# Convolution halves moved into the outer turns of a window attention, and the attention leads of TensorE's program set to one offset in a block of 256 instructions

## The chip, the cores and the metric

One core of one Trainium2 chip runs the whole program. The metric is the time of an execution on the device in microseconds (us). TensorE (PE), VectorE (DVE), ScalarE (ACT), GpSimd (POOL) and SyncE (SP) each run a program of their own and meet only in semaphores.

## The reference, cut to what matters

Eight images of 256 channels and 56 x 56 pixels go through two layers, both of the form `x = x + f(group_norm(x))`, in float32:

```
x = x + conv3x3(gn(x))                       # 256 -> 256 channels
qkv    = einsum('nchw,oc->nohw', windows(gn(x)), qkv_w)   # windows of 4 x 4 pixels
pooled = 5 x 5 average of qkv inside the window
q, k   = relu(q), relu(k) ; v = [v, 1]       # 32 + 32 heads of 8, plain and pooled
kv     = einsum('ngld,nglm->ngdm', k, v)
out    = einsum('ngld,ngdm->nglm', q, kv) ; out = out[..., :-1] / out[..., -1:]
x = x + batch_norm(einsum('nchw,oc->nohw', out, proj_w))
```

## The kernel before

**Convolution.** An image is cut into 4 chunks of 14 rows (`c`). Along a row the 3 taps become 4 products (`kk`, Winograd's F(2,3)), so an image has 16 steps; `v = 16 * image + 4 * c + kk` numbers them. A step is two halves (`mt`, output channels 0 to 127 and 128 to 255); `product(v, mt)` (L320) issues one half: 18 matmuls of 128 x 392 on split float32 operands. VectorE forms the step's input `dt` (`product_inputs`), ScalarE rounds it to `dp`'s high part (`split`), VectorE subtracts for the low part (`low_parts`), and later adds the half from PSUM to the image (`add_product`, semaphore `conv_added`). `conv_bank` (L87) names each half's PSUM bank.

**Attention.** An image has 196 windows, 8 to a tile, so 25 tiles. `attention(b)` runs 25 turns, s = 0 to 24. In turn s TensorE (`tile`, L417) does: `attend` of tile s (64 small float32 matmuls, issued as 128 pairs of a weight load and a matmul); `keys_times_values` of tile s+1 (64 pairs); `q_of_tile` of tile s+2 (8 pairs); `turn`, four transposes of tile s, after VectorE's `outputs`; `pooled` of tile s+2 (2 pairs, after VectorE's `kv_low_part`); `project` of tile s-1 (16 pairs, after VectorE's `mask`); `keys_values` of tile s+3 (6 pairs). The first and the last turns leave out what has no tile. Turns 1 to 20 are a hardware loop (`pe.Fori`) of two turns a pass; turn 0 ahead of it and turns 21 to 24 behind it are written out, and so is all convolution.

**How the two are woven.** The first chunk of the next image's convolution (steps 0 to 3) is issued by `first_chunk(b)` between the group norm and the first small products of image b's attention: a part of this, from `product(v + 3, 0)` to the entry of the loop, is called the lead here. Two halves of the next step, (c, kk) = (1, 0), stand in turns 23 and 24, where `q_of_tile` has nothing to do. The remaining halves follow in `later_chunks`. The last image's attention has no convolution beside it. VectorE's and ScalarE's programs have the same weave in `first_chunk`, `attention` and `later_chunks`.

**Instruction slots.** A pair of a weight load and a matmul is two instructions. Waits that do not fit on one are instructions of their own: some 7 in a turn, the loop's own included. From one lead to the next TensorE's program as written has 4,238 instructions, and 4,238 = 16 x 256 + 142.

**Loads.** SP stores each image row group when its tiles are added, and after row group 11 (all tiles to 20 are in) it loads the image after next into the freed rows.

Of the kernel before, what the change touches and what calls it, by code (L numbers as in the profile page):

```python
# [76 lines left out]
BANK_Q = 0  # L77
# [9 lines left out]
def conv_bank(v, mt):  # L87

    c, kk = v // len(PRODUCTS) % CONV_CHUNKS, v % len(PRODUCTS)
    if (c, kk) == (0, len(PRODUCTS) - 1):  # L90
        return BANK_O + mt
    if (c, kk) == (1, 0):
        return (BANK_Q, BANK_KV)[mt]
    return BANK_C[kk % 2][mt]
# [23 lines left out]
FIRST_LOOPED = 1  # L118

# [11 lines left out]
def build(nc, x, w_conv, w_q, w_kv, w_proj, bn, gavg, pool_m, ident, hmask, vinit, out):  # L131
    ctx = ExitStack()
    with ctx:
# [182 lines left out]
        def _(pe):  # L316
# [101 lines left out]
            def tile(T, e, s=None, v=None):  # L418
# [30 lines left out]
                if is_tile(2):  # L449
                    pe.wait_ge(q_ready, n2)  # L450
                    q_of_tile(e)
                if v is not None and not is_tile(2):
                    if is_tile(1):
                        pe.wait_ge(q_ready, n2)
                        product(v, 0)
                    else:
                        pe.wait_ge(vp_raw, n1)
                        product(v, 1)
                pe.wait_ge(ao_ready, n1)
                turn(units(0))  # L460
                if is_tile(2):
                    pooled(n3)
                if is_tile(-1):
                    if is_tile(1):
                        pe.wait_ge(masked, own_mask)
                    else:
                        pe.wait_ge(y_ready, n0)
                    project(1 - e, 2)
                if is_tile(3):
                    pe.wait_ge(xh_low, n4)  # L470
                    pe.wait_ge(vp_raw, n3)
                    keys_values(n4, 1 - e)
# [9 lines left out]
            def attention(b):  # L482
                t0 = b * TILES
                v = (b + 1) * CONV_STEPS + len(PRODUCTS) if b + 1 < B else None
                pe.wait_ge(q_ready, t0 + 1)
                q_of_tile(1)
                if b + 1 == B:
                    first_keys_times_values(b)
                pe.wait_ge(xh_low, t0 + 3)
                pe.wait_ge(vp_raw, t0 + 2)  # L490
                keys_values(t0 + 3, 0)
                if b + 1 < B:
                    pe.wait_ge(conv_added, 2 * v + 4)
                for s in range(FIRST_LOOPED):
                    tile(t0 + s, s % 2, s)
                with pe.Fori(0, LOOPED // 2) as i:
                    for e in range(2):
                        tile(t0 + i * 2 + (FIRST_LOOPED + e), (FIRST_LOOPED + e) % 2)
                for s in range(FIRST_LOOPED + LOOPED, TILES):
                    tile(t0 + s, s % 2, s, v)  # L500
# [17 lines left out]
            def later_chunks(b):  # L518

                for c in range(1, CONV_CHUNKS):
                    for kk in range(len(PRODUCTS)):
# [3 lines left out]
                        if b >= 1 and (c, kk) == (1, 2):  # L526
                            pe.wait_ge(y_ready, b * TILES + 1)
                        product(v, 0)
                        if b >= 1 and (c, kk) == (1, 1):
                            last_tile(b - 1)  # L530
# [6 lines left out]
            def first_chunk(b):  # L537
# [12 lines left out]
                second_tile(b)  # L550
                product(v + 3, 0)
# [3 lines left out]
                product(v + 3, 1)  # L555
# [30 lines left out]
        def _(act):  # L586
# [73 lines left out]
            def attention(b):  # L660
                for s in range(-1, TILES):
                    if s >= 0:
                        turned(b, s)
# [22 lines left out]
            def first_chunk(b):  # L686
# [13 lines left out]
                split(v + 5)  # L700
# [37 lines left out]
        def _(dve):  # L738
# [104 lines left out]
            def later_chunks(b):  # L843
                for c in range(1, CONV_CHUNKS):
                    for kk in range(len(PRODUCTS)):
                        v = b * CONV_STEPS + c * len(PRODUCTS) + kk
                        at = (c, kk) if b + 1 < B else None
                        low_parts(v + 1)
# [19 lines left out]
            def first_chunk(b):  # L868
# [36 lines left out]
                add_product(v + 3, 1)  # L905
# [65 lines left out]
            def attention(b):  # L971
                normalize_tile(b, 3)
                tile_low(b, 3)
                for s in range(TILES):
                    weights(b, s)
                    outputs(b, s)
                    if s + 2 < TILES:
                        kv_low_part(b, s + 2)
                    if s + 1 < TILES:
                        mask(b, s + 1, 0)  # L980
                        mask(b, s + 1, 1)
                        pooled_q(b, s + 1)
                    if s + 4 < TILES:
# [225 lines left out]
```

## Time and profile before

| | |
|---|---|
| median of 3 executions | 2502.22 us (2491.29 to 2502.49) |
| the profiled execution's own time | 2488.01 us |
| its span, first to last instruction | 2486.1 us |
| TensorE busy | 2389.9 us, 96% |
| VectorE busy | 1970.8 us, 79% |
| ScalarE, GpSimd busy | 1280.5 us, 1169.2 us |
| TensorE's mean granted clock | 0.994 of full |

The profiled execution is 0.6% under the median of the three others and 0.1% under the fastest of them. Busy time is that in which an instruction of the engine was running by the record.

### The profile page before, as it was taken

Reading aid. Unit: us, or ns where it says so; the run is one execution under the profiler, and the core shown is the slowest. Engines: PE = TensorE matmul, PEld = TensorE weight load, DVE = VectorE, ACT = ScalarE, POOL = GpSimd, SP = SyncE. Lnnn points to the kernel's source line nnn. Section 1 sums busy time; section 2 is a strip of 40 time slices with the busy share of each in tenths; the row PEclk is TensorE's granted clock in tenths of the full one; section 3 lists DMA queues with packets and bytes.
Section 4 is the critical chain, followed back from the end, with each engine's and each line's share of the span. In section 5 each row is a group of like instructions: output and inputs, shape, how many; then the busy total and the mean of one; then the engine's idle time right before and its main releaser. Section 6 shows DMA issues by size and latency. Waiting matters only on the chain.

```text
span 2486.1 us, 112351 instructions
## 1 busy us (share of the span) xinstructions
PE 2389.9 (96%) x49576; PEld 2162.7 (87%) x49576; DVE 1970.8 (79%) x3608; ACT 1280.5 (52%) x3352; POOL 1169.2 (47%) x2364
## 2 busy tenths in 40 slices
PE   4999999999999999999999999999999999999998
PEld 4998889888898888988889888898889978898887
DVE  8887868888688886878858788687886878865886
ACT  2137751377514774157731577316772267722775
POOL 0026760277503775047740477305772067712776
PEclk9999999999999999999999999999999999999999
DMA  4000010000100002000010000100001000000000
GB/s 166 1 2 14 17 61 16 2 16 15 65 12 2 16 19 72 1 2 19 19 68 1 6 15 19 69 1 6 19 15 69 1 9 15 21 11 2 16 15 24
DMA packets 38959, 58.19 MB, mean 23 GB/s; under 512 B 4688, under 2 KB 36304, under 8 KB 36560
## 3 DMA queue, kind: packets, MB, share of 16 engines
q1 hardware_dynamic: 38736, 55.27, 6.3%
q8 instruction: 133, 2.18, 0.4%
q14 instruction: 90, 0.74, 0.1%
HBM read 29.57 MB, written 25.69 MB: 22 GB/s over the span
## 4 chain that ended last, share of the span: by engine, by line
PE 95%; issue 2%; DVE 1%; ACT 0%; DMA 0%; POOL 0%; SPq 0%; POOLq 0%; DVEq 0%
PE ps L334 34%; PE ps L405 15%; PE ps L353 11%; PE ps L394 10%; PE ps L380 9%; PE ps L360 9%; PE ps L369 4%; PE ps L414 3%; DMA xs<-w_conv 0%; PE ps L319 0%; DVE st L772 0%; PE ps L561 0%; PE ps L345 0%; ACT ve L613 0%; DVE xh L914 0%
## 5 line engine op out<-in xcount | busy, mean ns | idle before, releaser
L334 PE MATMUL ps<-dp,wc 128*128 128x392 f32 x4608 | 844.7, 343 | 5.6 <-issue 5.6
L334 PEld LDWEIGHTS ps<-dp,wc 128*128 128x128 f32 x4608 | 821.0, 189 | 11.3 <-issue 9.7
L1138 POOL TENSOR_TENSOR ve<-vpraw,vmask 128x1024 f32<-128x1024 f32 x200 | 392.1, 1961 | 364.6 <-ACT vpraw L624 364.6
L405 PEld LDWEIGHTS ps<-at,wp 128*128 128x128 f32 x3200 | 376.3, 192 | 49.6 <-DVE kvm L954 46.3
L1109 POOL TENSOR_TENSOR qm<-qraw 128x64 f32<-128x64 f32 x200 | 59.5, 298 | 763.2 <-ACT qraw L631 763.2
L914 DVE TENSOR_SCALAR xh<-xs,gn 128x128 f32<-128x128 f32 (+3 forms) x560 | 407.9, 781 | 0.5 <-PE ps L360 0.2
L405 PE MATMUL ps<-at,wp 128*128 128x128 f32 (+1 forms) x3200 | 405.5, 280 | 1.0 <-ACT yb L647 1.0
L595 ACT CAST dp<-dt 128x896 fp32r<-128x896 f32 x128 | 120.9, 944 | 513.4 <-PE ps L334 423.6
L353 PE MATMUL ps<-wkv,xt 128*128 128x512 f32 x1200 | 324.6, 406 | 7.1 <-issue 7.1
L613 ACT ACTIVATE ve<-ps,vmask 128x256 f32<-128x256 f32 x800 | 314.2, 490 | 0.0
L833 DVE TENSOR_TENSOR xs<-xs,ps 128x392 f32<-128x392 f32 x384 | 201.1, 558 | 125.0 <-PE ps L334 124.2
L394 PEld LDWEIGHTS ps<-kvm,qs 64*32 64x32 f32 x25088 | 232.2, 105 | 77.5 <-issue 74.8
L655 ACT COPY at<-ps 128x256 f32<-128x256 f32 (+1 forms) x400 | 128.3, 371 | 310.6 <-PE ps L414 310.4
L954 DVE TENSOR_TENSOR kvm<-ps,hm 128x576 f32<-128x576 f32 (+1 forms) x400 | 278.8, 737 | 11.6 <-PE ps L380 11.5
L380 PE MATMUL ps<-ve,kr 64*32 64x144 f32 x12544 | 253.5, 286 | 32.6 <-issue 32.6
L394 PE MATMUL ps<-kvm,qs 64*32 64x36 f32 x25088 | 256.8, 204 | 7.8 <-issue 7.4
L1149 POOL TENSOR_TENSOR xs<-yb,xs 128x128 f32<-128x128 f32 (+3 forms) x560 | 200.9, 386 | 107.9 <-ACT yb L647 107.9
L353 PEld LDWEIGHTS ps<-wkv,xt 128*128 128x128 f32 x1200 | 211.6, 189 | 45.8 <-issue 11.0
L360 PEld LDWEIGHTS ps<-xh,wq 128*128 128x128 f32 x1600 | 195.7, 192 | 44.2 <-issue 43.5
L360 PE MATMUL ps<-xh,wq 128*128 128x128 f32 x1600 | 231.7, 288 | 1.8 <-issue 1.8
L380 PEld LDWEIGHTS ps<-ve,kr 64*32 64x32 f32 x12544 | 193.8, 105 | 41.4 <-issue 41.1
L647 ACT ACTIVATE yb<-ps,bns,bni 128x128 f32<-128x128 f32 (+1 forms) x400 | 160.5, 452 | 91.7 <-PE ps L405 89.4
(87 smaller groups left out, 2898.9 us busy)
## 6 DMA issues: line engine op xcount, KB each, us to landing
out<-xs SPq DMA_DIRECT2D x224, 112.0 KB, 1.8
xs<-x SPq DMA_DIRECT2D x16, 1344.0 KB, 9.7
xs<-x SPq DMA_DIRECT2D x16, 224.0 KB, 2.7
xs<-w_conv SPq DMA_DIRECT2D x1, 2304.0 KB, 9.0
kvm<-w_kv SPq DMA_DIRECT2D x1, 512.0 KB, 14.2
wp<-w_proj SPq DMA_DIRECT2D x4, 128.0 KB, 7.8
wq<-w_q SPq DMA_DIRECT2D x1, 256.0 KB, 14.1
gav<-gavg SPq DMA_DIRECT2D x1, 64.0 KB, 8.7
```

Of the source, the lines that this page charges most:

```text
L334: last = nc.tensor.matmul(ps[:, conv_bank(v, mt), 0:CONV_N], wc[:, part_w, k, kt * TAPS + dy, mt * P:(mt + 1) * P], dp[:, kk % 2, part_d, ...
L353: last = nc.tensor.matmul(ps[0:TT, BANK_KV, :], xt[:, part_x, e, kt, :], wkv[:, part_w, kt, :], start=(i == 0 and kt == 0), stop=(i == len ...
L360: last = nc.tensor.matmul(ps[:, BANK_Q, mt * TT:(mt + 1) * TT], wq[:, kt, mt * P:(mt + 1) * P], xh[:, e, kt, :], start=(kt == 0), stop=(kt ...
L380: last = nc.tensor.matmul(ps[32 * q:32 * q + 32, BANK_A + 2 * h + r, gg * PLACES * QW:(gg + 1) * PLACES * QW], kr[64 * r:64 * r + 64, e, k ...
L394: last = nc.tensor.matmul(ps[32 * c:32 * c + 32, BANK_O + r, (u * G + g) * QW:(u * G + g + 1) * QW], qs[64 * r:64 * r + 64, g, e, w * 32:w ...
L405: last = nc.tensor.matmul(ps[:, BANK_A + mt, Y0:Y0 + n], wp[:, q, mt * P:(mt + 1) * P], at[:, q, e, 0:n], start=(q == 0), stop=(q == QUADS ...
L613: last = nc.scalar.activation(ve[:, t % 2, e, 0].rearrange("p (n m) -> p n m", m=DIM + 1)[:, :, 0:DIM], ps[0:TT, BANK_KV, C:2 * C].rearran ...
L833: last = nc.vector.tensor_tensor(pair[:, :, e], pair[:, :, e], ps[:, conv_bank(v, mt), 0:CONV_N], op)
L914: last = nc.vector.tensor_scalar(xh[:, t % 2, kt, first * TOK:(first + n) * TOK].rearrange("p (w r c) -> p w r c", r=WS, c=WS), xs_row(b, ...
L954: nc.vector.tensor_tensor(kvm[:, h, 0:n].rearrange("p r (g c) -> p r g c", g=2), ps[:, BANK_A + 2 * h:BANK_A + 2 * h + n, 0:2 * PLACES * Q ...
L1138: nc.gpsimd.tensor_tensor(ve[:, t % 2, :, 1].rearrange("p e (n m) -> p e n m", m=DIM + 1)[:, :, :, 0:DIM], vpraw[:].rearrange("p (n m) -> ...
L1149: last = nc.gpsimd.tensor_tensor(xrow, yb[:, t % 2, mt, first * TOK:(first + n) * TOK].rearrange("p (w r c) -> p w r c", r=WS, c=WS), xrow ...
```

## The change

- In `attention(b)` with an image to follow, four convolution halves stand in turns 0, 22, 23 and 24, where two stood in turns 23 and 24. Turn 0 has the second half of step (0, 3), taken out of `first_chunk`; turn 22 has the first half of step (1, 0), turn 23 its second, turn 24 the first half of step (1, 1), whose second half opens `later_chunks`.
- In turn 0 the half stands where `q_of_tile` stood; `q_of_tile` comes behind `pooled` and waits for that half's `add_product`, since both use BANK_Q. In turn 22 the half stands behind `project`.
- `conv_bank` gives these halves other banks.
- ScalarE's `split` for step (1, 1) moves into turn 1, VectorE's `low_parts` for it into turn 2, ahead of `kv_low_part`; VectorE's `add_product` of step (0, 3)'s second half moves into turn 0.
[...]

```diff
@@ -87,10 +87,12 @@
 def conv_bank(v, mt):
 
     c, kk = v // len(PRODUCTS) % CONV_CHUNKS, v % len(PRODUCTS)
+    if v < CONV_STEPS:
+        return BANK_C[kk % 2][mt]
     if (c, kk) == (0, len(PRODUCTS) - 1):
-        return BANK_O + mt
+        return (BANK_O, BANK_Q)[mt]
     if (c, kk) == (1, 0):
-        return (BANK_Q, BANK_KV)[mt]
+        return (BANK_KV, BANK_Q)[mt]
     return BANK_C[kk % 2][mt]
 
 
@@ -116,6 +118,7 @@
 STATS_AT = {(1 + (i + 1) // 4, (i + 1) % 4): i for i in range(CHUNKS)}
 LOOPED = TILES - 5
 FIRST_LOOPED = 1
+LEAD_SLOT = 152
 
 
 def gn0_of(img):
@@ -446,26 +449,33 @@
                     pe.wait_ge(vp_ready, n2)
                     keys_times_values(1, 1 - e, units(1))
 
-                if is_tile(2):
+                half = None if v is None else {0: (v - 1, 1), TILES - 3: (v, 0), TILES - 2: (v, 1),
+                                               TILES - 1: (v + 1, 0)}.get(s)
+                if half and s == 0:
+                    pe.wait_ge(q_ready, n2)
+                    product(*half)
+                elif is_tile(2):
                     pe.wait_ge(q_ready, n2)
                     q_of_tile(e)
-                if v is not None and not is_tile(2):
-                    if is_tile(1):
-                        pe.wait_ge(q_ready, n2)
-                        product(v, 0)
-                    else:
-                        pe.wait_ge(vp_raw, n1)
-                        product(v, 1)
+                elif half:
+                    pe.wait_ge(q_ready, n2 if is_tile(1) else n1)
+                    product(*half)
                 pe.wait_ge(ao_ready, n1)
                 turn(units(0))
                 if is_tile(2):
                     pooled(n3)
+                if half and s == 0:
+                    pe.wait_ge(conv_added, 2 * v + 4)
+                    q_of_tile(e)
                 if is_tile(-1):
                     if is_tile(1):
                         pe.wait_ge(masked, own_mask)
                     else:
                         pe.wait_ge(y_ready, n0)
                     project(1 - e, 2)
+                if half and s == TILES - 3:
+                    pe.wait_ge(vp_raw, n3)
+                    product(*half)
                 if is_tile(3):
                     pe.wait_ge(xh_low, n4)
                     pe.wait_ge(vp_raw, n3)
@@ -490,9 +500,9 @@
                 pe.wait_ge(vp_raw, t0 + 2)
                 keys_values(t0 + 3, 0)
                 if b + 1 < B:
-                    pe.wait_ge(conv_added, 2 * v + 4)
+                    pe.wait_ge(conv_added, 2 * v + 3)
                 for s in range(FIRST_LOOPED):
-                    tile(t0 + s, s % 2, s)
+                    tile(t0 + s, s % 2, s, v)
                 with pe.Fori(0, LOOPED // 2) as i:
                     for e in range(2):
                         tile(t0 + i * 2 + (FIRST_LOOPED + e), (FIRST_LOOPED + e) % 2)
@@ -523,11 +533,12 @@
                         v = b * CONV_STEPS + c * len(PRODUCTS) + kk
                         if b >= 1 and (c, kk) == (1, 0):
                             continue
-                        if b >= 1 and (c, kk) == (1, 2):
+                        if b >= 1 and (c, kk) == (1, 1):
+                            product(v, 1)
+                            last_tile(b - 1)
                             pe.wait_ge(y_ready, b * TILES + 1)
+                            continue
                         product(v, 0)
-                        if b >= 1 and (c, kk) == (1, 1):
-                            last_tile(b - 1)
                         if b + 1 < B and (c, kk) == (CONV_CHUNKS - 1, 1):
                             group_sum(gn0_of(b + 1), 1)
                         product(v, 1)
@@ -548,11 +559,11 @@
                 pooled(b * TILES + 1)
                 product(v + 2, 1)
                 second_tile(b)
+                pe.addr_align(bass.FETCH_BLOCK_INSTRUCTIONS, offset=LEAD_SLOT, max_nops=0)
                 product(v + 3, 0)
                 pooled(b * TILES + 2)
                 pe.wait_ge(conv_added, 2 * (v + 3) + 4)
                 first_keys_times_values(b)
-                product(v + 3, 1)
 
             pe.wait_ge(gav_loaded, DMA)
             for s in range(2):
@@ -659,6 +670,8 @@
 
             def attention(b):
                 for s in range(-1, TILES):
+                    if s == 1 and b + 1 < B:
+                        split((b + 1) * CONV_STEPS + len(PRODUCTS) + 1)
                     if s >= 0:
                         turned(b, s)
                     if 0 <= s < TILES - 2:
@@ -697,7 +710,6 @@
                 split_tile(b, 2)
                 keys_values(b, 1)
                 pooled_keys_values(b, 1)
-                split(v + 5)
 
             act.wait_ge(bn_step, 1)
             nc.scalar.activation(bnt[:, 1, :], bnt[:, 0, :], ACT.Sqrt).then_inc(bn_ready, 1)
@@ -845,7 +857,8 @@
                     for kk in range(len(PRODUCTS)):
                         v = b * CONV_STEPS + c * len(PRODUCTS) + kk
                         at = (c, kk) if b + 1 < B else None
-                        low_parts(v + 1)
+                        if b == 0 or (c, kk) != (1, 0):
+                            low_parts(v + 1)
                         if at == (CONV_CHUNKS - 1, 1):
                             group_means(gn0_of(b + 1), gn0)
                         if at == (CONV_CHUNKS - 1, 2):
@@ -902,7 +915,6 @@
                 mask(b, 0, 0)
                 mask(b, 0, 1)
                 pooled_q(b, 0)
-                add_product(v + 3, 1)
 
             def normalize_tile(b, t):
 
@@ -971,15 +983,20 @@
             def attention(b):
                 normalize_tile(b, 3)
                 tile_low(b, 3)
+                v = (b + 1) * CONV_STEPS + len(PRODUCTS)
                 for s in range(TILES):
                     weights(b, s)
                     outputs(b, s)
+                    if s == 2 and b + 1 < B:
+                        low_parts(v + 1)
                     if s + 2 < TILES:
                         kv_low_part(b, s + 2)
                     if s + 1 < TILES:
                         mask(b, s + 1, 0)
                         mask(b, s + 1, 1)
                         pooled_q(b, s + 1)
+                    if s == 0 and b + 1 < B:
+                        add_product(v - 1, 1)
                     if s + 4 < TILES:
                         normalize_tile(b, s + 4)
                         tile_low(b, s + 4)
```

## Rows read from the trace of the kernel before

**Rows 1.** Page, part 4: chain that ended last, by engine.

```profile
PE 95%; issue 2%; DVE 1%; ACT 0%; DMA 0%; POOL 0%; SPq 0%; POOLq 0%; DVEq 0%
```

**Rows 2.** TensorE's waits: who, until what, us in total, times, longest us.

```profile
PE ps L380 <- issue: 32.6, 21, 4.4
...
PE ps L394 <- issue: 7.4, 7, 1.5
PE ps L353 <- issue: 7.1, 9, 0.8
```

**Rows 3.** Page, part 3: queue of TensorE's instructions: packets, MB, share.

```profile
q8 instruction: 133, 2.18, 0.4%
```

**Rows 4.** Fifth attention, lead to turn 2, TensorE in order of time: start, us.

```profile
1383.74 3.36 PE L334 MATMUL ps<-dp,wc 128*128 128x392 f32 x18
...
1398.59 0.44 PE L380 MATMUL ps<-ve,kr 64*32 64x144 f32 x4 [1.68 <-issue]
...
1401.81 1.62 PE L353 MATMUL ps<-wkv,xt 128*128 128x512 f32 x6 [0.79 <-issue]
1403.36 1.06 PE L394 MATMUL ps<-kvm,qs 64*32 64x36 f32 x101
1405.97 0.35 PE L394 MATMUL ps<-kvm,qs 64*32 64x36 f32 x27 [1.54 <-issue]
...
1414.55 0.25 PE L394 MATMUL ps<-kvm,qs 64*32 64x36 f32 x2 [0.57 <-issue]
```

**Rows 5.** DMA view of 1394 to 1402 us: busy tenths in 40 slices of 0.2 us.

```profile
DMA  0000000003000000000000000000000000000000
```

**Rows 6.** Windows: first, fifth, sixth attention, lead to turn 24; sum of seven.

```profile
167.50:381.35 213.85, 206.42 (x5672) 179.14 (x5670) 168.00 (x302) 139.95 (x387) 139.84 (x285) 0.98 0.08 28
...
1383.74:1595.37 211.63, 203.69 (x5672) 176.20 (x5670) 169.18 (x302) 139.63 (x387) 139.79 (x285) 1.00 0.08 28
1686.87:1895.91 209.04, 203.32 (x5671) 176.14 (x5670) 166.73 (x302) 139.64 (x387) 140.11 (x285) 1.00 0.08 29
...
sum 1482.64, PE 1435.02 PEld 1243.52 DVE 1176.28 ACT 978.18 POOL 979.37; mean PE 205.00 PEld 177.65 DVE 168.04 ACT 139.74 POOL 139.91
```

**Rows 7.** Window of turns 3 to 20 of the fourth attention.

```profile
1114.75:1252.48 137.73, 137.73 (x4105) 117.90 (x4104) 121.02 (x212) 103.26 (x288) 104.56 (x215) 1.00 0.05 17
```

**Rows 8.** Fifth attention, turns 21 to 23, TensorE in order of time.

```profile
1562.69 0.95 PE L380 MATMUL ps<-ve,kr 64*32 64x144 f32 x42 [1.82 <-issue]
...
1572.32 0.55 PE L380 MATMUL ps<-ve,kr 64*32 64x144 f32 x17 [1.47 <-issue]
...
1578.83 3.47 PE L334 MATMUL ps<-dp,wc 128*128 128x392 f32 x18
```

**Rows 9.** Fourth attention, turn 23, TensorE in order of time.

```profile
1267.45 0.93 PE L380 MATMUL ps<-ve,kr 64*32 64x144 f32 x22
1272.80 1.16 PE L380 MATMUL ps<-ve,kr 64*32 64x144 f32 x10 [4.42 <-issue]
1273.89 5.27 PE L334 MATMUL ps<-dp,wc 128*128 128x392 f32 x18
```

**Rows 10.** Window in that turn: DMA share and GB/s are the last two.

```profile
1267.00:1275.00 8.00, 3.58 (x107) 2.74 (x94) 2.82 (x7) 0.22 (x1) 3.81 (x11) 0.75 0.82 331
```

**Rows 11.** A turn in the loop, VectorE and TensorE in order of time.

```profile
1734.49 0.68 DVE L927 TENSOR_TENSOR kv_part<-ps,kv_part 128x512 fp32r<-128x512 f32 x1
...
1735.08 1.41 DVE L954 TENSOR_TENSOR kvm<-ps,hm 128x576 f32<-128x576 f32 x2
...
1735.35 0.71 PE L369 MATMUL ps<-kv_part,poolm 128*128 128x512 f32 x2
...
1735.89 2.04 PE L405 MATMUL ps<-at,wp 128*128 128x128 f32 x16
```

**Rows 12.** Tile dp: ns of the low part on VectorE, min/median/max.

```profile
L820 DVE TENSOR_TENSOR dp<-dt,dp x128: 1028/1084/1140, 37.3 to 2254.9; 128x896 fp32r<-128x896 f32 x128
```

**Rows 13.** Page, part 5: adding a half to the image.

```profile
L833 DVE TENSOR_TENSOR xs<-xs,ps 128x392 f32<-128x392 f32 x384 | 201.1, 558 | 125.0 <-PE ps L334 124.2
```

## Prediction

> **What bounds the kernel now.** I read the chain that ended last first: 95% of the span is TensorE's own work and 2% "issue" [rows 1]. So time can come only from TensorE's idle places or slow stretches. TensorE's waits come next [rows 2]: the largest in the three small-matmul lines name no other engine but "issue", 32.6 us in 21 places ahead of L380, 7.4 us ahead of L394, 7.1 us ahead of L353. The third kind is regular, 0.79 us in each attention, in turn 0 between `pooled` and `keys_values` [rows 4]; there is no `project` in turn 0 to cover ScalarE's reading of the bank, whose end (`vp_raw`) `keys_values` needs.
>
> The other two look random until they are counted in instructions. In the fifth attention TensorE stops after 60 of the 64 pairs of turn 0's `keys_times_values` (4 follow the stop), next after 101 pairs of turn 1's `attend` [rows 4]. Between the stops lie 4 + 8 + 4 + 2 + 6 + 101 = 125 pairs, 250 instructions, and 6 waits: 256. To the stop at 1414.55 it is 27 + 64 + 8 + 4 + 2 + 16 + 6 + 126 = 253 pairs and 6 waits: 512. So TensorE stops where a block of 256 instructions ends. Queue q8 brought 133 packets, 2.18 MB, or 16 KB each [rows 3]: 64 bytes times 256. Before the stop that ended at 1398.59 one packet went at 1395.8 to 1396.0 [rows 5], 2.6 us earlier.
>
> Where does it hurt? 128 `attend` pairs take 1.15 us, so blocks made of `attend` and `keys_times_values` are used up in some 1.5 to 2 us. A block start lies 125 pairs ahead of a stop; from there to the resumption it is 3.1 to 3.5 us for the stops of turns 0, 21 and 22 of the fifth attention [rows 4, 8]. One is much later: 1398.59 to 1405.97, 7.4 us, where the block began some 50 instructions ahead of the loop's entry [rows 4]. Another sort stands in the fourth attention's turn 23: 1266.5 to 1272.8, 6.3 us, of which 4.42 us idle [rows 9], while the DMA engines were 82% busy with the next load [rows 10]; behind it the 18 convolution matmuls took 5.1 us for 3.3, at half the granted clock for a part (mean 0.75 in that window) [rows 9, 10]. Inside the loop nothing is fetched again: 18 turns ran without idle time [rows 7].
>
> **The change, part by part.** The reference is the stretch from the lead to the end of turn 24 and its following half. Seven of them take 1482.64 us, 211.8 on average, between 209.04 (sixth) and 213.85 (first), with the same work [rows 6].
>
> *The offset.* Counting back from 1398.59, two blocks and 106 instructions, the lead of the fifth attention stands 151 instructions behind a block start; the change puts all seven at 152. From there to turn 21 the counts of pairs are as before (half (0, 3, 1) moves, within the lead, behind turn 0's `keys_times_values`). So the fifth attention, 211.63 us, is the model, and only what moves is taken off it. The jump over the padding (114 slots, from the spacing of 142) stays in one block; 9 jumps per attention back to the loop's head show no idle time [rows 7]. I take 0.
>
> *Turn 0.* In the model a block start fell after 60 pairs of `keys_times_values`, 1.68 us idle [rows 4]. With the half gone from ahead of it the block start falls some 78 pairs into `attend` of turn 0, and the block before it holds `q_of_tile` and `keys_values`: some 3.7 us of work against 3.1 to 3.5. Gain 1.68. The next block start then lies 12 matmuls into the moved half, 4.2 us on: no stop.
>
> *`q_of_tile` behind `pooled`.* It covers the 0.79 us [rows 4], but waits for the half's adding, 0.56 us on VectorE [rows 13], behind which VectorE has masks and, early in the attention, a tile's normalization still queued. Bounds 0 and 0.8 us of new wait; I take 0.4: gain 0.39.
>
> *Turn 1.* The stop of 1.54 us [rows 4] belongs to the late packet at the loop's entry. Now 6.3 us of work (6 matmuls, `turn`, `pooled`, `q_of_tile` with its wait, `keys_values`, 101 pairs) stand ahead of it. A packet in 3.5 us gives no stop, one in 7.4 us 1.1 us. I take the middle, 0.5: gain 1.04. The 0.57 us in turn 2 stays.
>
> *`low_parts` in turn 2.* 1.08 us [rows 12], ahead of `kv_low_part`. In a turn of the loop `kv_part` ends at 1735.17 and `pooled` starts at 1735.35; the first half of the mask ends near 1735.8 and `project` starts at 1735.89 [rows 11]. There is 0.1 us of slack, so nearly all goes on TensorE's path: loss 1.0, bounds 0.9 and 1.1. ScalarE's `split` in turn 1 falls in a time when it waits for the transposes: 0, and if it were not hidden about 0.9 once.
>
> *Turns 21 and 22.* Nothing is moved ahead of their stops, 1.82 and 1.47 us [rows 8]: unchanged.
>
> *Turns 22 to 24.* A half of 3.3 us [rows 8] now stands in each of turns 22, 23, 24. Block starts fall, by pairs, near the 60th pair of `attend` of turn 23 and then 3 pairs into its `project`, with 0.6 + 1.1 + 3.3 + 0.4 + 0.3 = 5.7 us between them. The load runs here. At 6.2 us for a packet beside it [rows 9] the stop is 0.5; without a delay 0. I take 0.45. The fifth attention had none here.
>
> *VectorE behind the attention.* The half taken out of `later_chunks` leaves 5 us (two halves and less) ahead of step (1, 2) after turn 24, in which VectorE must form and split its input; by the order of its work it is done some 2 us early. 0.
>
> Sum: 211.63 - 1.68 - 0.39 - 1.04 + 1.0 + 0.45 = 209.97; seven, 1469.8 against 1482.6: 12.8 us less. The last attention is not aligned itself but moves by some 27 instructions within its block (its loop's entry from 4 past a block start to about 23 short of one). Its stops are of the same sizes, up to 1.9 each, and one more or less can come: bounds -2 and +3; I take +1. In all 11.8 us off the profiled 2488.0, or 2476.2. Against the median of 2502.2, which is 14.2 above that execution, 2490.4.
>
> [...] The rows above give 3.1 to 3.5 us per block against less than 2 us of small matmuls. [...]
>
> **Rivals.**
> - *Blocks are not what stops TensorE.* Then the offset does nothing: 7 x (1.0 - 0.39) = +4.3, 2506. Against it stand the counts of 256 and 512. [...] 0.05.
> - *The jump costs a packet.* 3.4 us, less 1.4 for the `keys_values` matmuls queued ahead of it: 2.0 x 7 = +14, 2504. Against it: no idle time at the loop's jumps [rows 7]. [...] 0.08.
> - *Slower: the load catches the packet in turn 23.* If the packet comes not 6.2 but 10 us after its block's start, as the load now falls on other work, the fourth attention's whole loss of 4.42 + 1.8 comes in six attentions: +5.8 x 6 = 35, 2525. It decides from 3.6 us per attention on, a packet at 9 us. For it: the fourth attention had it. Against it: it needs more than the latest packet above took, 7.4. 0.06.
> - *All late packets are hidden.* Turn 1, turn 23 and the add's wait go: 1.35 x 7 = 9.5 more, 2481. 0.13.
> - *The grid is off by some slots*, so that the stops of turns 21 and 22 shrink too: with half of their 3.3 us gone 11.5 more, or 2479; with all, 2468. 0.14.
> - *Every late packet stays late*: turn 1 at 1.1, 0.8 in turn 0, 0.7 in turn 23: +1.25 x 7, 2499. 0.06.
>
> **How the numbers follow.** My case has 0.48, its own range 2484 to 2497 by the middles taken above. What a measurement of this kernel can tell from no change is about 0.5%, 12.5 us. That bound, 2489.7, cuts my case nearly at its middle: 0.19 of it beyond, 0.29 within. Faster: 0.19 + 0.13 + 0.14 = 0.46. Same: 0.29 + 0.05 + 0.08 + 0.06 = 0.48. Slower: 0.06. The range 2470 to 2507 leaves out the load's case and the ends of the grid's.
>
> **What would show it.** In the profile of the changed kernel: "issue" ahead of L380 falls from 32.6 to about 26 us; turn 0 of the seven attentions has no stop in `keys_times_values` and no 0.79 us ahead of `keys_values`; the stops stand at the same pair in all seven; turn 2 is 1.0 us longer than turn 3, with `pooled` and `project` waiting for VectorE; turn 23 has at most one short stop in `project`, no half clock. Seven equal stretches near 210 us confirm the model; unequal ones refute the alignment. I am wrong if turn 2's delay is hidden, if turns 21 and 22 change, or if the load meets a block's packet.

## The result, and the profile after

The changed kernel takes 2491.1 us (median of 20 executions, 2483.3 to 2497.7), the kernel before 2497.5 us (20 executions, 2489.6 to 2502.5): ratio 0.9977, 95% interval 0.9968 to 0.9986. That is 6.4 us, or 0.2%. The interval leaves out 1, but the kernel before by itself had medians of 2492.8 and 2494.3 us at two other times, so a difference of this size is hardly more than no change. I had forecast 2490.4 us, and a gain of 11.8 us over the profiled execution. The profiled executions differ by 1.7 us only, 2488.0 before and 2486.3 after (spans 2486.1 and 2484.5). So the time was met and its sum was not; both parts of that are taken apart below.

Lines of the changed kernel are those of before plus 3 on TensorE (`keys_times_values` L380 is now L383, `attend` L394 is L397, and so on); on VectorE `kv_low_part`'s tile `kv_part` is L939, the mask L966, `qs` L977. Page, part 4 of the changed kernel, the chain that ended last, by engine (before: [rows 1]):

```profile
PE 89%; DVE 5%; issue 3%; ACT 2%; DMA 0%; POOL 0%; SPq 0%; POOLq 0%; DVEq 0%
```

DVE and ACT have come into the chain. TensorE's waits in the changed kernel: who, until what, us in total, times, longest us (before: [rows 2]):

```profile
PE ps L383 <- issue: 28.8, 17, 2.1
PE ps L397 <- issue: 7.6, 12, 1.0
PE ps L337 <- ACT yb L658: 5.6, 7, 0.8
PE ps L372 <- DVE kv_part L939: 5.5, 9, 0.8
PE ps L337 <- issue: 2.0, 1, 2.0
PE ps L397 <- DVE qs L977: 1.9, 8, 0.4
...
PE ps L356 <- issue: 1.6, 2, 0.8
```

"issue" is idle time for which the profile names no other engine. With its smaller lines it was 55.4 us before; now it is 28.8 + 7.6 + 2.0 + 1.6 = 40.0. That is 15.4 us less. Against it stand waits for other engines that were not there: 5.6 us for ScalarE's `yb`, 5.5 for `kv_part` (0.9 before) and 1.9 for `qs` (0.4 before), 11.7 more. Most of the stops that went were traded for waits.

Fifth attention, lead to turn 2, TensorE in order of time: start, us, instruction, idle time ahead of it (before: [rows 4]):

```profile
1382.94 1.29 PE L397 MATMUL ps<-kvm,qs 64*32 64x36 f32 x128 [0.23 <-DVE qs L977]
1384.07 1.23 PE L383 MATMUL ps<-ve,kr 64*32 64x144 f32 x64
1385.23 3.46 PE L337 MATMUL ps<-dp,wc 128*128 128x392 f32 x18
...
1390.61 1.63 PE L356 MATMUL ps<-wkv,xt 128*128 128x512 f32 x6
1392.17 1.06 PE L397 MATMUL ps<-kvm,qs 64*32 64x36 f32 x100
1394.26 0.35 PE L397 MATMUL ps<-kvm,qs 64*32 64x36 f32 x28 [1.03 <-issue]
...
1403.12 0.25 PE L397 MATMUL ps<-kvm,qs 64*32 64x36 f32 x3 [0.88 <-issue]
...
1406.60 0.74 PE L372 MATMUL ps<-kv_part,poolm 128*128 128x512 f32 x2 [0.60 <-DVE kv_part L939]
```

The 64 pairs of turn 0's `keys_times_values` run through, and the half follows them. `keys_values` (L356) has no idle time ahead of it. The stop in turn 1 comes after 100 pairs (101 before) and is 1.03 us. In turn 2 `pooled` waits for `kv_part`. The same attention's end:

```profile
1552.32 0.95 PE L383 MATMUL ps<-ve,kr 64*32 64x144 f32 x43 [2.06 <-issue]
...
1562.21 0.65 PE L383 MATMUL ps<-ve,kr 64*32 64x144 f32 x18 [1.74 <-issue]
...
1570.91 1.18 PE L383 MATMUL ps<-ve,kr 64*32 64x144 f32 x32
1572.02 3.47 PE L337 MATMUL ps<-dp,wc 128*128 128x392 f32 x18
...
1583.61 3.45 PE L337 MATMUL ps<-dp,wc 128*128 128x392 f32 x18
1586.90 1.89 PE L408 MATMUL ps<-at,wp 128*128 128x64 f32 x16
1589.59 2.58 PE L337 MATMUL ps<-dp,wc 128*128 128x392 f32 x13 [0.79 <-ACT yb L658]
```

The stops of turns 21 and 22 stand one pair from where they were, 21 and 46 pairs in (22 and 47 before, [rows 8]), and they stand at these pairs in all seven attentions. Turn 23 has none. The last row is new. From the last tile's `project` to the next convolution half it is 1589.59 - 1586.90 = 2.69 us, of which TensorE works 1.89; before, 1.70 us lay between such starts.

Windows of the changed kernel for its first, fourth and sixth attention (us, busy time of the engines, granted clock, DMA share, GB/s). Between the lead and the half behind the last `project` the changed kernel has one half more than the kernel before, so each window ends 3.3 us, the time of a half, ahead of where that half starts. Its length then compares with [rows 6]; its busy times do not, since the cut falls inside other work:

```profile
166.90:377.43 210.53, 204.81 (x5670) 177.03 (x5669) 167.03 (x299) 140.00 (x387) 140.32 (x285) 1.00 0.08 29
...
1074.41:1283.44 209.03, 204.84 (x5670) 176.96 (x5669) 167.11 (x299) 139.94 (x387) 141.43 (x285) 1.00 0.08 29
...
1677.89:1889.87 211.98, 206.22 (x5670) 178.43 (x5669) 167.21 (x299) 140.12 (x387) 140.34 (x285) 0.99 0.08 28
```

The seven are 210.53, 212.22, 209.97, 209.03, 211.25, 211.98 and 211.89: sum 1476.9 against 1482.6 before, 210.98 on average against a forecast of 209.97. The fourth, which had the stop beside the load, fell from 213.6 to 209.0; the sixth rose from 209.0 to 212.0. Outside them the changed kernel is 4.1 us longer: 2.6 from the last attention to the end, 1.6 ahead of the last attention, 0.6 in six convolutions, less 0.6 at the start.

The sixth shows what still differs from one attention to the next. TensorE in its turn 22, and a window behind the stop (the clock is the third value from the end):

```profile
1864.18 0.65 PE L383 MATMUL ps<-ve,kr 64*32 64x144 f32 x18 [1.74 <-issue]
1864.76 1.83 PE L363 MATMUL ps<-xh,wq 128*128 128x128 f32 x8
```

```profile
1864.00:1868.00 4.00, 3.82 (x32) 3.48 (x32) 1.75 (x4) 0.74 (x2) 0.00 (x0) 0.63 0.20 61
```

The stop is as long as in the fifth attention, 1.74 us, but the eight matmuls behind it take 1.83 us where the fifth has 1.16: the granted clock is at its lower level, 0.50 of full (window 1865.10 to 1868.50), for a while. Each such stretch in the seven attentions of the two traces lasts 3.41 us or twice that. By estimate, from the 0.50, one of 3.41 with TensorE busy throughout costs half of it, 1.7 us. The seven attentions of this execution have three. The kernel before had eight times 3.41 us in its seven. Windows laid on these stretches, before (the one beside the load, and the sum of all) and after (the sum):

```profile
1271.03:1277.86 6.83, 5.06 (x22) 4.51 (x23) 0.98 (x3) 0.00 (x0) 0.18 (x1) 0.50 0.45 185
...
sum 27.30, PE 24.39 PEld 22.83 DVE 7.28 ACT 4.52 POOL 1.99; mean PE 4.07 PEld 3.81 DVE 1.21 ACT 0.75 POOL 0.33
```

```profile
sum 10.23, PE 10.23 PEld 9.60 DVE 4.30 ACT 2.28 POOL 0.00; mean PE 3.41 PEld 3.20 DVE 1.43 ACT 0.76 POOL 0.00
```

Half of TensorE's busy time in them is what the lower clock cost, by estimate: 12.2 us before, 5.1 after. Without it the seven attentions take 1482.6 - 12.2 = 1470.4 us before and 1476.9 - 5.1 = 1471.8 after. By this estimate the 5.8 us by which the seven fell are all clock, and at an equal clock the changed kernel's are about 1.3 us longer.

### The profile page after: what moved, and what is told of

It is laid out like the page before. It is cut to its first block, busy times and chain, and to the rows that moved or that the text cites. A ratio compares the mean times of both kernels' runs of the same rounds, so it can differ in the third digit from the quotient of the medians.

```text
span 2484.5 us, 112358 instructions
## 1 busy us (share of the span) xinstructions
PE 2391.6 (96%) x49576; PEld 2159.6 (87%) x49576; DVE 1977.9 (80%) x3608; ACT 1282.2 (52%) x3352; POOL 1173.8 (47%) x2364
## 4 chain that ended last, share of the span: by engine, by line
PE 89%; DVE 5%; issue 3%; ACT 2%; DMA 0%; POOL 0%; SPq 0%; POOLq 0%; DVEq 0%
PE ps L337 31%; PE ps L408 15%; PE ps L356 10%; PE ps L397 9%; PE ps L363 8%; PE ps L383 8%; PE ps L372 4%; PE ps L417 3%; ACT ve L624 1%; DVE kvm L966 1%; DVE xh L926 1%; ACT kv_part L619 0%; DVE qs L977 0%; DVE kv_part L939 0%; PE ps L322 0%
## 5 line engine op out<-in xcount | busy, mean ns | idle before, releaser
L337 PE MATMUL ps<-dp,wc 128*128 128x392 f32 x4608 | 840.9, 341 | 7.6 <-ACT yb L658 5.6
L337 PEld LDWEIGHTS ps<-dp,wc 128*128 128x128 f32 x4608 | 815.3, 188 | 13.5 <-ACT yb L658 6.5
L926 DVE TENSOR_SCALAR xh<-xs,gn 128x128 f32<-128x128 f32 (+3 forms) x560 | 419.1, 800 | 1.6 <-PE ps L363 1.3
L356 PE MATMUL ps<-wkv,xt 128*128 128x512 f32 x1200 | 324.8, 406 | 1.6 <-issue 1.6
L397 PEld LDWEIGHTS ps<-kvm,qs 64*32 64x32 f32 x25088 | 232.7, 105 | 81.0 <-issue 79.2
L966 DVE TENSOR_TENSOR kvm<-ps,hm 128x576 f32<-128x576 f32 (+1 forms) x400 | 278.4, 736 | 10.3 <-PE ps L383 10.1
L383 PE MATMUL ps<-ve,kr 64*32 64x144 f32 x12544 | 251.9, 285 | 28.8 <-issue 28.8
L397 PE MATMUL ps<-kvm,qs 64*32 64x36 f32 x25088 | 257.4, 204 | 9.5 <-issue 7.6
L356 PEld LDWEIGHTS ps<-wkv,xt 128*128 128x128 f32 x1200 | 211.7, 189 | 37.3 <-issue 2.6
L383 PEld LDWEIGHTS ps<-ve,kr 64*32 64x32 f32 x12544 | 193.4, 105 | 36.6 <-issue 36.2
```

The lines of the kernel that those rows point to most:

```text
L337: last = nc.tensor.matmul(ps[:, conv_bank(v, mt), 0:CONV_N], wc[:, part_w, k, kt * TAPS + dy, mt * P:(mt + 1) * P], dp[:, kk % 2, part_d, ...
L356: last = nc.tensor.matmul(ps[0:TT, BANK_KV, :], xt[:, part_x, e, kt, :], wkv[:, part_w, kt, :], start=(i == 0 and kt == 0), stop=(i == len ...
L383: last = nc.tensor.matmul(ps[32 * q:32 * q + 32, BANK_A + 2 * h + r, gg * PLACES * QW:(gg + 1) * PLACES * QW], kr[64 * r:64 * r + 64, e, k ...
L397: last = nc.tensor.matmul(ps[32 * c:32 * c + 32, BANK_O + r, (u * G + g) * QW:(u * G + g + 1) * QW], qs[64 * r:64 * r + 64, g, e, w * 32:w ...
L926: last = nc.vector.tensor_scalar(xh[:, t % 2, kt, first * TOK:(first + n) * TOK].rearrange("p (w r c) -> p w r c", r=WS, c=WS), xs_row(b, ...
L966: nc.vector.tensor_tensor(kvm[:, h, 0:n].rearrange("p r (g c) -> p r g c", g=2), ps[:, BANK_A + 2 * h:BANK_A + 2 * h + n, 0:2 * PLACES * Q ...
```

## The experiments

The first four below ran beside 23 executions of the kernel before (median 2492.8 us), the last four at another time, on another chip, beside another 23 (2494.3). The eight have 12, 12, 6, 6, 12, 6, 10 and 4 executions. Each ratio is against the kernel before.

**1. The offset alone.** The kernel before, with only the alignment added:

```diff
                 second_tile(b)
+                pe.addr_align(bass.FETCH_BLOCK_INSTRUCTIONS, offset=152, max_nops=0)
                 product(v + 3, 0)
```

> The kernel before with nothing but the alignment of the seven leads to slot 152. Block theory (TensorE stops where a block of 256 instructions ends among small matmuls): every one of the seven attentions now looks like the fifth of before, 211.6 us, so the seven stretches take 1481 us against 1482.6, and the last attention, which comes to lie at another offset, is about 2.6 us longer as it was in the changed kernel: ratio to before 1.000 (0.998 to 1.002). Rival (the alignment is what made the changed kernel faster): ratio 0.997 or less.

2496.6 us, ratio 1.0011 (0.9996 to 1.0026): no gain, as expected. Its fifth attention, lead to turn 2:

```profile
1398.47 0.44 PE L380 MATMUL ps<-ve,kr 64*32 64x144 f32 x5 [1.63 <-issue]
...
1401.69 1.61 PE L353 MATMUL ps<-wkv,xt 128*128 128x512 f32 x6 [0.80 <-issue]
...
1405.57 0.35 PE L394 MATMUL ps<-kvm,qs 64*32 64x36 f32 x28 [1.27 <-issue]
...
1413.89 0.25 PE L394 MATMUL ps<-kvm,qs 64*32 64x36 f32 x3 [0.33 <-issue]
```

It is the pattern of [rows 4], one pair off, and the other six attentions now have it too: from the lead to the loop they take 19.3 to 20.0 us, where the attentions before varied from 17.8 to 20.0. So the model attention was read rightly, and it was one of the worse ones for its lead. The seven take 1486.9 us against 1481 expected, or 1480.2 without the lower clock's share, counted as above; that is 10 us more than the 1470.4 of before. The offset made the stops stand at the same places here; it did not make them few: "issue" takes 63.6 us in this kernel, 55.4 in the one before.

**2. The order alone.** The changed kernel without the `addr_align` line.

> The changed kernel without the alignment; leads fall 142 slots further each time, as before. Block theory: turns 1 and 2 of the seven attentions lose some 12 us against the changed kernel, turns 21 and 22 win some 17 us, turn 23 and the lead lose between 0 and 12 us: ratio to before 0.998, between 0.995 and 1.001, about the changed kernel's own. Stops move from attention to attention again. Rival (the alignment made the gain): ratio 1.000 to 1.003, clearly above the changed kernel's 0.9977.

2492.4 us, ratio 0.9990 (0.9974 to 1.0005). The stops wander again: turn 21 takes from 7.6 to 11.4 us. In the second and fourth attention one falls beside the load, in turn 23. TensorE in the second:

```profile
669.66 1.18 PE L383 MATMUL ps<-ve,kr 64*32 64x144 f32 x15 [2.88 <-issue]
670.77 5.90 PE L337 MATMUL ps<-dp,wc 128*128 128x392 f32 x18
```

A stop of 2.88 us, and a half at 5.90 us for 3.47: turn 23 takes 13.96 and 13.09 us in these two and 7.9 elsewhere, 11.3 us lost in all. The offset avoids that, but pays for it. Against the changed kernel, the leads and turns 1, 2 and 23 of the seven attentions are 27.5 us longer here, and turns 21 and 22 are 16.8 us shorter (turns 1 and 2 make 4.7 of it, where I had expected 12); the difference is about the lower clock's, 16.4 us here and 5.1 there. In the medians the two kernels cannot be told apart (2492.4 here, 2491.1 and 2492.3 for the changed kernel), as I had expected. No run shows that the offset made the changed kernel faster.

**3. The suspected wait taken away.** The half behind the last `project` gets another bank, and the wait for ScalarE's last reading stands where that bank is next needed:

```diff
     if (c, kk) == (1, 0):
         return (BANK_KV, BANK_Q)[mt]
+    if (c, kk) == (1, 2):
+        return BANK_O + mt
...
                             last_tile(b - 1)
-                            pe.wait_ge(y_ready, b * TILES + 1)
                             continue
+                        if b >= 1 and (c, kk) == (2, 0):
+                            pe.wait_ge(y_ready, b * TILES + 1)
```

> The changed kernel, with step (1, 2) in PSUM banks 2 and 3 instead of 4 and 5, so that the wait for ScalarE's reading of the last tile's projection stands only ahead of step (2, 0). Theory: the 0.98 us behind the last project in each of seven attentions goes, 6.9 us, ratio to before 0.9950 (0.9940 to 0.9962). Rival (TensorE only meets the same delay at a later step, VectorE being late with its inputs there): ratio stays at 0.9977.

2478.1 us, ratio 0.9928 (0.9906 to 0.9950). Fifth attention, the same place (here `project` is L410 and `product` L339):

```profile
1588.62 1.89 PE L410 MATMUL ps<-at,wp 128*128 128x64 f32 x16
1590.32 5.96 PE L339 MATMUL ps<-dp,wc 128*128 128x392 f32 x32
```

1.70 us from start to start instead of 2.69, in all seven, and the wait for `yb` at this place is gone from the list. From the start of turn 24 to that half it is 10.91 us for 11.90: 0.99 x 7 = 6.9 us shown, as expected. The ratio is below the range that I expected from this, 0.9940 to 0.9962; the section on the clock, below, takes this up.

**4. The low part moved to where VectorE is idle.** `low_parts` goes from turn 2 to turn 22, behind `pooled_q`; the half that needs it stands in turn 24:

```diff
-                    if s == 2 and b + 1 < B:
-                        low_parts(v + 1)
                     if s + 2 < TILES:
                         kv_low_part(b, s + 2)
...
+                    if s == TILES - 3 and b + 1 < B:
+                        low_parts(v + 1)
```

> The changed kernel, with VectorE's low_parts of step (1, 1) in turn 22 behind pooled_q instead of in turn 2 ahead of kv_low_part. Theory: turn 2 is 1.0 us shorter in each of seven attentions, turn 22 is no longer since a convolution half stands there: 7 us, ratio 0.9950 (0.9940 to 0.9962). Rival (the time is given back in turn 2 as a longer stop for the next block, since TensorE uses the block up sooner): turn 2 no shorter, ratio 0.997 to 0.998.

2476.8 us, ratio 0.9930 (0.9907 to 0.9953). VectorE in its fifth attention:

```profile
1557.61 0.23 DVE L947 TENSOR_SCALAR den<-ps 128x64 f32<-128x64 f32 x1 [4.91 <-PE ps L397]
...
1561.73 1.09 DVE L832 TENSOR_TENSOR dp<-dt,dp 128x896 fp32r<-128x896 f32 x1
1568.75 0.23 DVE L947 TENSOR_SCALAR den<-ps 128x64 f32<-128x64 f32 x1 [5.94 <-PE ps L397]
```

VectorE has 4.9 us idle ahead of turn 22 and still 5.9 behind the low part, so its 1.09 us cost nothing there: turns 22 and 23 take 11.66 and 7.90 us on average, 11.60 and 7.90 in the changed kernel. Turn 2 takes 7.9 to 8.4 us, 8.09 on average, where the changed kernel has 9.30: 1.2 us each, 8.5 in all. The wait for `kv_part` falls from 5.5 to 0.9 us. So turn 2 is not given back as a longer stop. The ratio is again below the range expected, 0.9940 to 0.9962.

**5. The changed kernel again**, beside the next three.

> The changed kernel itself, beside the kernels of this call. Both theories: ratio 0.9977 (0.996 to 0.9995).

2492.3 us, ratio 0.9983 (0.9966 to 1.0001).

**6. Both edits.**

> The changed kernel with both edits: step (1, 2) in banks 2 and 3 with the wait ahead of step (2, 0), and low_parts of step (1, 1) in turn 22. Theory (two separate places on TensorE's path): the last project of each of seven attentions is 1.0 us shorter and turn 2 is 1.2 us shorter; 15 us off the changed kernel, ratio 0.9915 (0.990 to 0.993), faster than the kernel before and than either edit alone. Rival (both win the same slack once): as either alone, 0.993 to 0.995.

2474.6 us, ratio 0.9925 (0.9901 to 0.9949), 17.7 us under the changed kernel beside it. It has the lowest time of all. The two edits alone had already given 0.9928 and 0.9930, so by the medians they do not add. In experiment 3 the wait taken away is 6.9 us by the trace, and the median lies 13.0 us under the changed kernel's 2491.1, taken at another time: more than its cause can give.

**7. Another offset:** `LEAD_SLOT = 180`, 28 slots (14 pairs) on.

> The changed kernel with the leads at slot 180 instead of 152. Block theory, by the seventh attention of the kernel without the alignment, whose lead falls at 179: in all seven attentions the stop of turn 21 shrinks from 2.2 to 0.3 us, that of turn 22 stays at 1.3 to 1.8, turn 1 has none in attend, and turn 0 gets one of some 1.8 us at the start of its convolution half, followed by 1.5 us at half clock: each stretch 0 to 1.5 us longer or shorter, ratio 0.996 to 1.000. Rival (stops belong to places in the program, not to offsets): the stops stay at the same pairs as at 152.

2487.1 us, ratio 0.9976 (0.9958 to 0.9994). TensorE in the fifth attention, turns 0, 22 and 23:

```profile
1388.31 1.23 PE L383 MATMUL ps<-ve,kr 64*32 64x144 f32 x64
1391.72 3.45 PE L337 MATMUL ps<-dp,wc 128*128 128x392 f32 x18 [2.18 <-issue]
...
1562.69 0.73 PE L383 MATMUL ps<-ve,kr 64*32 64x144 f32 x32
1565.04 0.72 PE L383 MATMUL ps<-ve,kr 64*32 64x144 f32 x32 [1.62 <-issue]
...
1574.92 2.59 PE L337 MATMUL ps<-dp,wc 128*128 128x392 f32 x13
1579.24 1.04 PE L337 MATMUL ps<-dp,wc 128*128 128x392 f32 x5 [1.73 <-issue]
```

The stop of turn 22 comes after 32 pairs instead of 46, 14 earlier, as 28 slots ask. A stop of 1.5 to 2.2 us is back in turn 0, behind its 64 pairs, in all seven, and one beside the load in turn 23, in five of them. Turn 21 has at most 0.3 us. All this is where I expected it; the lower clock that I expected behind turn 0's stop did not come (the half there takes 3.45 us), and turn 22's stop, 1.6 to 2.2 us, is somewhat longer than the 1.3 to 1.8 expected. "Issue" ahead of L383 falls from 28.8 to 16.1 us and rises ahead of L337 from 2.0 to 19.7. The places moved with the offset; the sum, 40.0 us in both, did not.

**8. The padding walked instead of jumped:** `addr_align` without `max_nops=0`, so that its padding, 58 NOPs (instructions that do nothing) ahead of the first lead and 256 - 142 = 114 ahead of the others, runs.

> The changed kernel with the padding run through as no-operations instead of jumped over (58 in the first attention, some 114 in the others). If the jump costs a packet of instructions, this kernel is faster by up to 14 us (0.992). If the jump is hidden, as the profile of the changed kernel says, it is the same, or slower by what 114 no-operations take beyond the matmuls queued ahead (1.4 us): with 10 to 30 ns for one, 0 to 2 us each, 0 to 14 us in all, 0.998 to 1.003.

2530.6 us, ratio 1.0150 (1.0119 to 1.0181), 38.4 us over the changed kernel beside it. I had expected 0 to 14 us, with 10 to 30 ns for a NOP. No run shows these; the trace gives at least 43. TensorE at the first and the fourth lead:

```profile
168.12 3.43 PE L337 MATMUL ps<-dp,wc 128*128 128x392 f32 x18 [0.64 <-issue]
...
1086.48 1.54 PE L356 MATMUL ps<-wkv,xt 128*128 128x512 f32 x6
1092.94 5.55 PE L337 MATMUL ps<-dp,wc 128*128 128x392 f32 x18 [4.92 <-issue]
```

4.92 us for 114 NOPs, at least 43 ns each, and the half behind them 5.55 us for 3.4 (mean granted clock 0.58 from 1092.90 to 1098.40). At the first lead, with 58, the idle time is 0.64 us. If the matmuls queued ahead hide as much in both places, 56 more NOPs cost 4.3 us: by this estimate some 75 ns each. The list has 32.1 us of "issue" ahead of L337 where the changed kernel has 2.0. The jump in the changed kernel shows no idle time at the same place, in any of the seven.

## Why the time was right and the sum was not

**The anchor and the sum missed in opposite directions.** Sum: 2476.2 forecast for the execution, 2486.3 measured, 10.1 too low. Anchor: the 14.2 us between the median of three and the profiled execution; over 20 executions it was 9.5 before, and 4.9 after. 9.3 too high. That 2490.4 lies so near 2491.1 is luck. Of gain by the medians, 11.8 us were forecast and 6.4 measured.

**The step that failed in the sum** is "*VectorE behind the attention* ... 0". I looked there for VectorE's lateness with step (1, 2) and found none, which holds. What I did not weigh was the diff's other effect at the same place. Before, half (1, 1, 1), 3.3 us of it, stood between the last `project` and the wait for `y_ready`; the change brings the wait directly behind `project`, and ScalarE's reading of the bank lies open. 0.98 us in each of seven attentions is 6.9 us; experiment 3 took 0.99 back in each.

**A larger error stands in what the sum was compared with.** I took 7 x 209.97, worked out from an attention with no lower clock, from the measured 1482.6, which has 12.2 us of lower clock in it. Without them the seven before take 1470.4 us, 210.1 each, and my model, at 211.6, was one of the longer ones. So the forecast of 12.8 us less, 1469.8, had 0.6 us by the edits and 12.2 by a clock that it did not mention (the shares of the clock are the estimates worked out above). Measured, without the clock's share, are 1471.8: 2.0 us over the forecast. The other 5.1 of the miss in these seven are the changed kernel's own lower clock.

The terms of the sum, in us per attention:

| term | forecast | mean of seven |
|---|---|---|
| lead to loop (model 19.62 - 1.68 - 0.39) | 17.55 | 17.13 |
| turn 1 (9.33 - 1.04) | 8.29 | 8.42 |
| turn 2 (8.37 + 1.0) | 9.37 | 9.30 |
| turns 3 to 20 | 137.97 | 137.96 |
| turn 21 | 9.70 | 10.05 |
| turn 22 with its half (7.83 + 3.3) | 11.13 | 11.60 |
| turn 23 (7.88 + 0.45) | 8.33 | 7.90 |
| behind the last `project` | 0 | 0.98 |

- *Turn 0:* right, stop and 0.79 us both gone. The add's wait (0.4 taken) is hardly there: 0.1 us ahead of `q_of_tile`. A new wait of 0.23 us for `qs` stands at the lead's `attend` instead. The whole is 0.4 better than forecast.
- *Turn 1:* right as a middle. Four attentions stop for about 1 us (turn 1 at 8.7 to 8.8), three not at all (7.9).
- *Turn 2:* right in sum. Experiment 4 gives 8.09 us without the move and 1.2 for it, where 8.37 and 1.0 were taken. The two misses cancel. The stop in `attend` lies between 0.16 and 0.88 us, 0.57 in the model.
- *Turns 21 and 22:* the stops are about unchanged, 1.73 and 1.70 us on average for 1.82 and 1.47. The excess, 0.82 x 7 = 5.7 us, is nearly all the three stretches at the lower clock, 3 x 1.7 = 5.1. The model attention had none ([rows 6], clock 1.00), and I had given them no term.
- *Turn 23:* no stop; 0.45 was too much. The load did no harm at this offset; beside it TensorE stopped in experiment 2, and in experiment 7.
- *The rest of the program:* +1 forecast, +4.1 measured. One stretch at the lower clock stands ahead of the last attention and one in its last turns, 3.4 us of it.

**The signs.** "Issue" ahead of the line of `keys_times_values` was to fall to about 26 us and fell to 28.8. The stops stand at the same pairs in all seven, as forecast. The stretches were to be near 210 us and equal; they go from 209.0 to 212.2, or 209.0 to 211.3 without the lower clock. I had called unequal stretches a refutation of the alignment. They are not one: the places are equal, the lengths of the stops are not (turn 21: 1.40 to 2.06 us). In turn 2 `pooled` waits for VectorE, `project` does not.

**The theories.** That stops stand at block ends is shown: experiment 1 reproduces one attention's pattern six times more, experiment 7 shifts it by 14 pairs for 28 slots. The rival by which blocks stop nothing is refuted by the same. That this jump costs a packet is refuted by the changed kernel's leads, which show no idle time at it; it stays within one block, so a forward jump into another block was not tried. How much of a step into the next block shows depends here on the work beside it: among the small matmuls of turns 21 and 22 it is a stop of 2.06 and 1.74 us in the fifth attention; in convolution, with 3.3 us of work in 36 instructions, the changed kernel has one place of "issue" in the whole program, 2.0 us ahead of L337, 46.6 us after the start. That the load catches the packet did not happen. "All late packets are hidden" fits turn 23 and three of seven turns 1, which have no stop.

**Where the expected gain went.** Summing waits, "issue" gave back 15.4 us and other waits took 11.7. Experiments 3 and 4 show that two of them cost 6.9 and 8.5 us of TensorE's path, and that the change did not need either. And 12.2 of the 12.8 us that the sum promised were not in the edits, but in the lower clock of the execution that it was compared with.

**What the clock has to do with the medians.** For 134 executions the span and the mean granted clock are on record. Within a kernel, 0.001 of mean clock goes with about 2.5 us of span. That is what the stretches ask: one costs 1.7 us and lowers the mean over 2490 us by 0.5 x 3.41 / 2490 = 0.00068. Carried by this slope to a clock of 0.996, mean spans are as below. The last column comes from the profiled execution alone: its seven attentions without the lower clock's share, counted as above.

| kernel | mean clock | span at 0.996 | seven attentions |
|---|---|---|---|
| before (two times) | 0.9924, 0.9923 | 2482.9, 2482.7 | 1470.4 |
| changed, first and second time | 0.9942, 0.9940 | 2484.6, 2483.7 | 1471.8, 1469.7 |
| offset alone | 0.9946 | 2491.1 | 1480.2 |
| order alone | 0.9931 | 2483.2 | 1470.0 |
| free banks | 0.9960 | 2476.4 | 1463.0 |
| late low part | 0.9957 | 2474.8 | 1461.8 |
| both edits | 0.9948 | 2470.6 | 1457.7 |
| offset 180 | 0.9965 | 2486.8 | 1472.6 |

Seen so, against the changed kernel's second time, the edits of experiments 3 and 4 give 7.3 and 8.9 us and both together 13.1 (8.2, 9.8 and 14.0 against its first): near the 6.9 and 8.5 that the traces show singly, and near their sum. The last column says the same: 7.7, 9.0 and 13.0 us under the mean of the changed kernel's two. And the changed kernel itself is not shown to be faster than the one before at an equal clock: its spans are 0.9 to 1.8 us longer, its seven attentions 1.4 longer and 0.7 shorter. Its 0.2% matches the time at the lower clock that it has less of, 0.0018 x 2.5 us per 0.001 = 4.5 us. The table leaves out experiment 8. Every other kernel with the leads aligned has a mean clock of 0.9940 or more, the two without 0.9931 or less. Both columns are accounts of executions, with differing numbers of them, and no experiment: they argue the split and do not show it. Why one stop is followed by the lower clock and the same stop in another attention is not, stays open; no experiment held the clock still.

## What to carry to other kernels

When a reordering takes work from between an instruction and a wait, ask of each wait that moves up what now stands ahead of it: here a semaphore that cost nothing behind 3.3 us of matmuls cost 0.98 us directly behind its producer. Aligning the leads made the stops of turns 21 and 22 repeat at the same pairs in all seven attentions, which gives a model that can be multiplied. But by itself it gained nothing here (ratio 1.0011, experiment 1). So choose the offset for where the stops fall, and place the edits that go with it in engines' idle time: one that was not took 1.2 us of turn 2 in each attention (experiment 4). Before one execution's total is compared with a sum of parts, take the time at the lower clock out of both: here it was 12.2 us, by estimate, of the 12.8 that the sum promised.

## What the runs showed of the hardware that was not expected

- The changed kernel's two profiled spans differ by 6.3 us, 2484.5 and 2490.8. The second has six stretches of 3.41 us at the lower clock, 0.50 of full, in its seven attentions, the first three, and the last attention adds to that. In the first, the clock fell behind stops of 1.64, 1.74 and 1.96 us and not behind others of 1.74, 2.00 and 2.06.
- A NOP on TensorE took at least 43 ns, 4.92 us for 114 of them, and some 75 ns by the estimate in experiment 8, where a jump over the same 114 slots showed no idle time.
- The loop ran through many times the instructions of a block without one stop in turns 3 to 20, in every trace: in the kernel before, 8,209 matmuls and weight loads in 18 turns ([rows 7]), in which q8 brought no packet. Meanwhile straight code of the same matmuls, turns 21 and 22 of the changed kernel, stopped for 1.4 to 2.1 us where, by the count, a block of 256 instructions ended among them.
- At the same offset and with the same work, turn 1 has its stop in four of seven attentions (1.03 us in the fifth) and none in three. What makes the difference was not tried.
